# Products of constants ahead of the sorts and the sets on TensorE

## The chip, the cores and the metric

The kernel runs on one core of one Trainium2 chip. The metric is the device time of one execution in microseconds (us). The engines are named as in the profile: PE is TensorE (PEld its weight loads), DVE VectorE, ACT ScalarE, POOL GpSimd, SP SyncE, which issues most DMAs. PE's clock is granted at one of two levels, 2.4 GHz (1.00 in the profile) and 1.2 GHz (0.50).

## The reference

Two transformer layers over x of 8 x 256 x 256. Layer 0 is a cross attention over a context, a self attention and a mixture of eight experts; layer 1 is a cross attention and a second expert layer, which is the part around the change. In it, tokens are taken in groups of 32; in each group each of 128 (expert, set) pairs chooses one token, that token runs through a small two-layer net of the pair, and the results are added back to the tokens:

```python
logits = einsum('bntd,des->bntes', grouped, Wc) + bc
logits = logits + tie
perm = (logits == max(logits, axis=-3, keepdims=True))
permuted = einsum('bntd,bntes->bnesd', grouped, perm)
inner = relu(einsum('bnesd,esdf->bnesf', permuted, W1) + b1)
result_permuted = einsum('bnesf,esdf->bnesd', inner, W2) + b2
result = einsum('bnesd,bntes->bntd', result_permuted, perm)
```

Here n counts the groups (64 in all with the batch), t the 32 tokens of one, e and s the 128 pairs, d the 256 features and f the 32 features of the small net.

## The kernel before

It is one program of five instruction streams, one for each engine, which meet through semaphores. A list of steps, worked out once, gives the order; each engine runs through the list and does its share of each step. So the order on PE is fixed: an instruction that waits holds up all that stand behind it. The rows of x are worked on in blocks of two tiles of 128 rows, eight blocks per attention, numbered 0 to 7, 8 to 15 and 16 to 23 over the three attentions.

The steps around the change, in the order of the program:

- The last attention (blocks 16 to 23) ends, for each block, with p1 (L850, spreads the inverse sums), p2 (`project_out`, L861 in f32 and L863 in bf16), a layernorm on DVE and POOL, ft (`front_turn`, L954, transposes it), fw (`front_choice`, L963, the choice logits), fm (three DVE operations that find the maxima) and fp (`perm_turn`, L971, transposes the choice). ACT copies the results of ft, fw and fp. In the list `last_order` these steps of the last two blocks, 22 and 23, stand between the sorts.
- `sort(b, k)`, gp in the list, b = 0 to 7, k = 0, 1: it gathers the chosen rows of block b by 24 products of 32 rows (L991), in two passes of 12; the second pass waits for the first (`wait_ge("gp", done + 2)`). It writes one of two buffers of PSUM, `PS`, in turn. Two copies (gc, 512 columns each) bring a buffer to G in SBUF; for b below 2 ACT makes both (L1217), else ACT one and DVE the other (L1568). A sort waits until the copies of the sort two before it have freed its buffer.
- `sets_up(b)`, e1, b = 0 to 3: 128 products of 128 rows by 32 columns (L1007) into one of three banks MB. It waits for all copies of the sorts. DVE adds the bias (L1574), ACT applies relu.
- `sets_down(n)`, e2, n = 0 to 7: 64 products of 32 rows (L1029) into four banks, even n into `PS`, odd n into U and MB. DVE (L1584) and ACT (L1229) copy them out; group n waits for the copies of group n - 2, which used its banks.
- Then transposes (L1042) and the products that add the results back (L1053).

The kernel has products of constants elsewhere: `keep_busy`, L1069, a matrix product of two constant tiles into `PS[0]`, behind steps listed by hand, among them eight behind the last `sets_down`. `idb` is the identity in bf16, `lo` a bf16 constant of 128 x 256; both are in SBUF long before the sorts. A `Gate` leaves out a wait that the engine has passed already.

Of the kernel before, what the change touches and what calls it, by code (L numbers as in the profile page):

```python
# [192 lines left out]
def down_on(g, j):  # L193


    return "a" if j == 0 or j == 1 and g in (0, 2, 4) else "b"


def downs(engine, g):

    return sum(down_on(i, j) == engine for i in range(g + 1) for j in range(4))
# [80 lines left out]
def count(what, *key):  # L282
    return NO[what][key]


def copies(engine, b, k):

    return sum(copy_on(*s[1:]) == engine for s in STEPS if s[0] == "gc" and s[1:3] <= (b, k))
# [47 lines left out]
BANKS = Ring(3, bank_users())  # L336
# [97 lines left out]
def build(nc, D, out, stack):  # L434
# [39 lines left out]
    idb = g0.new("idb", [128, 128], BF)  # L474
    vec = g0.new("vec", [128, 160])
    cst = g0.new("cst", [128, 176])
    lo = g0.new("lo", [128, 2, 128], BF)
# [145 lines left out]
    def set_bank(g, j):  # L623

        return ((U, MB[0], MB[1], MB[2])[j][:, :] if g % 2 else PS[j // 2][:, 512 * (j % 2):512 * (j % 2) + 512])
# [23 lines left out]
    def bank(*step):  # L649
        return MB[BANKS.of[step]]  # L650

    def pair(*step):
        return PS[PAIRS.of[step]]
# [70 lines left out]
    def tensor(e):  # L724
        g = Gate(e, sems)
# [240 lines left out]
        def perm_turn(n):  # L966
# [4 lines left out]
                i = e.transpose(b[:, 128 * tt:128 * tt + 128], perm[:, 8 * p + 4 * tt:8 * p + 4 * tt + 4, :], idf[:, :])  # L971
            i.then_inc(sems["pt"], 1)

        def sort(b, k):
            ps, done = pair("gp", b, k), 4 * (count("gp", b, k) - 1)
            g.wait_ge("perm_turned", b + 1)
            g.wait_ge("f_turned", 2 * (b + 1))
            g.wait_ge("fz", b + 1)
            g.wait_ge("fl", b + 1)
            for signal in PAIRS.free["gp", b, k] or ():  # L980
                g.free(signal)

            for pair_of in ((0, 2), (1, 3)):
                if pair_of[0]:
                    g.wait_ge("gp", done + 2)
                for tt in range(2):
                    t = 2 * b + tt
                    for part in range(3):
                        z = z2[:, t, :] if part == 2 else z01[:, t, part, :]
                        for r in pair_of:  # L990
                            i = e.matmul(ps[:, 512 * (r // 2) + 256 * (r % 2) + 128 * tt:][:, 0:128],  # L991
                                         z[32 * r:32 * r + 32, 128 * k:128 * k + 128], pT[32 * r:32 * r + 32, t, :],
                                         start=part == 0, stop=part == 2)
                            if (tt, part) == (1, 2):
                                i.then_inc(sems["gp"], 1)

        def sets_up(b):
            m = bank("e1", b)
            g.wait_ge("d_v1", 16)
            g.wait_ge("sorted_a", copies("a", 7, 1))  # L1000
            g.wait_ge("sorted_b", copies("b", 7, 1))
            g.free(BANKS.free["e1", b])
            for q in range(8):
                for j in range(4):
                    s = 16 * (2 * b + q // 4) + 4 * j + q % 4
                    for k in range(2):
                        i = e.matmul(m[32 * j:32 * j + 32, 64 * q:64 * q + 64], v1[:, k, s, :], G[:, k, s, :],  # L1007
                                     start=k == 0, stop=k == 1)
            i.then_inc(sems["e1"], 1)

        def sets_down(n):
            b, half = GROUPS[n] // 2, GROUPS[n] % 2
            banks = [set_bank(n, j) for j in range(4)]
            g.wait_ge(f"d_v2{(0, 1, 2, 0)[b]}", 32 if b in (0, 3) else 16)
            g.wait_ge("relu", b + 1)
            if n == 0:
                g.wait_ge("sorted_a", copies("a", 7, 1))
                g.wait_ge("sorted_b", copies("b", 7, 1))
            elif n == 1:
                g.wait_ge("up", 4)  # L1020
                g.wait_ge("u_copied", 48)
            else:
                g.wait_ge("down", downs("b", n - 2))
                g.wait_ge("down_a", downs("a", n - 2))

            for q in range(4):
                for k in range(2):
                    for j in range(4):
                        i = e.matmul(banks[j][:, 128 * q + 64 * k:128 * q + 64 * k + 64],  # L1029
                                     v2[32 * j:32 * j + 32, 4 * GROUPS[n] + q, 128 * k:128 * k + 128],  # L1030
                                     Tmp[b][32 * j:32 * j + 32, 4 * half + q, :], start=True, stop=True)
                        if (q, k) == (3, 1):
                            i.then_inc(sems["e2"], 1)
# [911 lines left out]
    with nc.Block() as block:  # L1945
        block.tensor(tensor)
        block.scalar(scalar)
        block.vector(vector)
        block.gpsimd(gpsimd)
        block.sync(sync)  # L1950
# [100 lines left out]
```

## Time and profile before

| | us |
|---|---|
| median of 3 runs | 826.19 |
| the runs | 825.30 to 828.41 |
| the profiled execution | 823.46 |
| its span | 821.5 |

All times below are from the profiled execution, counted from the start of its span. "Busy" counts the time an engine's instructions take; the granted clock is the mean over a stretch; the stage table has the engines in the order PE, PEld, DVE, ACT, POOL. In a timeline, equal instructions in a row are merged: start, time from the first one's start to the last one's end, engine, line, operation, what it writes and reads, shape and count; in brackets the engine's idle time just before and what ended it. "issue" there means that the engine waited for nothing that the profile shows. An f32 product of the program stands as two instructions in the trace. Products overlap, so the time of a merged row holds the last one's own latency.

### The profile page before, as it was taken

Reading aid. Unit: us, or ns where it says so; the run is one execution under the profiler, and the core shown is the slowest. Engines: PE = TensorE matmul, PEld = TensorE weight load, DVE = VectorE, ACT = ScalarE, POOL = GpSimd, SP = SyncE. Lnnn points to the kernel's source line nnn. Section 1 sums busy time; section 2 is a strip of 40 time slices with the busy share of each in tenths; the row PEclk is TensorE's granted clock in tenths of the full one; section 3 lists DMA queues with packets and bytes.
Section 4 is the critical chain, followed back from the end, with each engine's and each line's share of the span. In section 5 each row is a group of like instructions: output and inputs, shape, how many; then the busy total and the mean of one; then the engine's idle time right before and its main releaser. Section 6 shows DMA issues by size and latency. Waiting matters only on the chain.

```text
span 821.5 us, 17575 instructions
## 1 busy us (share of the span) xinstructions
PE 715.4 (87%) x6672; PEld 547.8 (67%) x6672; DVE 469.9 (57%) x1206; ACT 363.3 (44%) x671; POOL 251.6 (31%) x320
## 2 busy tenths in 40 slices
PE   8777988889988999887999999989887887888898
PEld 6544655556666666577988899977655565555775
DVE  4757777777788798571221221224557677746375
ACT  4355656445656655602232322210454546545233
POOL 6722434323443321212120210005433434332140
PEclk9988999999999999999999999999979899977899
DMA  9697666755654584339647476502658363043302
GB/s 192 100 208 133 109 89 93 94 93 94 86 84 78 82 184 148 143 129 325 229 115 244 120 239 192 182 20 69 103 93 121 54 91 54 29 169 162 106 16 90
DMA packets 60534, 101.90 MB, mean 124 GB/s; under 512 B 7278, under 2 KB 50734, under 8 KB 55440
## 3 DMA queue, kind: packets, MB, share of 16 engines
q1 hardware_dynamic: 58020, 95.29, 51.1%
q0 software_dynamic: 1872, 5.11, 3.1%
q8 instruction: 54, 0.88, 0.5%
q10 hardware_dynamic: 560, 0.38, 0.2%
q14 instruction: 28, 0.23, 0.1%
HBM read 55.22 MB, written 7.21 MB: 76 GB/s over the span
## 4 chain that ended last, share of the span: by engine, by line
PE 52%; DVE 18%; ACT 8%; DMA 5%; issue 5%; POOL 5%; another core or an unknown queue 3%; SPq 3%; ACTq 0%; POOLq 0%; DVEq 0%
PE MB L754 8%; PE PS L934 8%; PE U L945 7%; DVE nma L1339 5%; PE MB L861 5%; PE U L837 4%; PE MB L796 3%; PE MB L777 3%; DMA mw<-in_mw 2%; PE PS L819 2%; SPq L1820 2%; PE MB L1042 2%; PE PS L991 2%; DVE nmb L1339 1%
## 5 line engine op out<-in xcount | busy, mean ns | idle before, releaser
L1339 DVE TENSOR_REDUCE nma<-MB 128x2 f32<-128x512 f32 (+1 forms) x192 | 122.2, 671 | 38.5 <-PE MB L796 38.5
L1157 ACT ACTIVATE Pa<-PS 128x1024 f32<-128x1024 f32 (+1 forms) x96 | 97.8, 1025 | 32.9 <-PE PS L819 31.5
L934 PE MATMUL PS<-mzT,mw 128*128 128x128 f32 x736 | 86.3, 276 | 3.9 <-DMA mw<-in_mw 3.9
L945 PE MATMUL U<-mw,mdT 128*128 x368 | 85.3, 386 | 4.6 <-DVE mdT L1531 2.3
L796 PE MATMUL MB<-QKa 99*128 99x120 bf16 (+1 forms) x512 | 70.9, 250 | 19.2 <-DVE nma L1339 4.9
L934 PEld LDWEIGHTS PS<-mzT,mw 128*128 128x128 f32 x736 | 84.1, 192 | 5.0 <-DMA mw<-in_mw 4.9
L1539 DVE TENSOR_TENSOR yt<-U,mb 128x256 f32<-128x256 f32 x23 | 9.8, 424 | 131.7 <-PE U L945 131.7
L945 PEld LDWEIGHTS U<-mw,mdT 128*128 128x128 f32 x368 | 69.4, 194 | 14.3 <-issue 5.6
L796 PEld LDWEIGHTS MB<-QKa 99*128 99x128 bf16 x512 | 37.7, 100 | 50.8 <-DVE nma L1339 13.5
L1632 POOL TENSOR_TENSOR mv<-mv,vec 128x2 f32<-128x2 f32 (+1 forms) x40 | 30.6, 765 | 113.9 <-DVE mv L1296 62.0
L819 PE MATMUL PS<-QKa 101*128 101x256 bf16 (+1 forms) x384 | 58.8, 277 | 2.1 <-DMA QKa<-mTa 2.1
L837 PE MATMUL U<-Pa,Vaa 128*32 128x256 f32 (+1 forms) x768 | 56.9, 399 | 2.0 <-ACT Pa L1157 2.0
L1179 ACT ACTIVATE mzT<-MB,vec 128x128 f32<-128x128 f32 x46 | 18.6, 456 | 88.7 <-PE MB L918 88.7
L1676 POOL DMA_INDIRECT zt<-hb,rows_of x23 | 22.0, 956 | 109.7 <-PE MB L918 97.8
L754 PE MATMUL MB<-zTa,W 128*128 128x256 f32 x192 | 48.3, 396 | 6.6 <-ACT zTa L1095 3.5
L1641 POOL TENSOR_TENSOR rqa<-tqa,spa 128x512 f32<-128x512 f32 (+1 forms) x28 | 32.4, 1158 | 69.0 <-ACT tqa L1136 46.4
L1339 DVE TENSOR_REDUCE nmb<-MB 128x4 f32<-128x480 f32 x64 | 39.8, 645 | 18.0 <-PE MB L796 17.3
L819 PEld LDWEIGHTS PS<-QKa 101*128 101x128 bf16 (+1 forms) x384 | 38.5, 112 | 9.9 <-issue 3.5
L754 PEld LDWEIGHTS MB<-zTa,W 128*128 128x128 f32 x192 | 35.3, 194 | 14.3 <-ACT zTa L1095 4.3
L1648 POOL TENSOR_TENSOR spa<-rqa,spa 128x512 bf16<-128x512 f32 (+1 forms) x28 | 32.6, 1163 | 33.2 <-ACT spa L1144 33.0
L1157 ACT ACTIVATE Pb<-PS 120x1024 f32<-120x1024 f32 x32 | 32.8, 1026 | 14.0 <-PE PS L819 13.8
L1189 ACT ACTIVATE mdT<-PS,vec 128x128 f32<-128x128 f32 x92 | 26.4, 372 | 28.4 <-PE PS L934 28.0
(227 smaller groups left out, 1388.3 us busy)
## 6 DMA issues: line engine op xcount, KB each, us to landing
mw<-in_mw SPq DMA_DIRECT2D x31, 1024.0 KB, 6.5
QKa<-spa SPq DMA_DIRECT2D x144, 128.0 KB, 4.8
Qb<-spb SPq DMA_DIRECT2D x48, 128.0 KB, 4.3
Oa<-Uba SPq DMA_DIRECT2D x16, 256.0 KB, 2.6
v<-in_v SPq DMA_DIRECT2D x1, 4096.0 KB, 13.4
v<-in_v SPq DMA_DIRECT2D x4, 1024.0 KB, 10.6
yb<-yt SPq DMA_DIRECT2D x23, 128.0 KB, 1.7
QKa<-spa SPq DMA_DIRECT2D x24, 120.0 KB, 4.0
```

The source lines that it names most:

```text
L754: i = e.matmul(b[:, 256 * half:256 * half + cols], w[:, k, 128 * half:128 * half + 128], rhs[:, k, :], start=k == 0, stop=k == 1)
L796: i = e.matmul(b[:, keys * j:keys * j + keys], Q[0:99, h0 + j, 128 * qt:128 * qt + 128], K[0:99, h0 + j, 0:keys], start=True, stop=True)
L819: i = e.matmul(ps[0:keys, c:c + 256], K[0:101, h, keys * kt:keys * kt + keys], Q[0:101, h, :], start=True, stop=True)
L837: i = e.matmul(U[32 * j:32 * j + 32, 256 * gg:256 * gg + 256], V[0:keys, kt, 8 * half + 4 * gg + j, :], p[0:keys, c:c + 256], start=kt == ...
L861: e.matmul(b[:, 256 * tt:256 * tt + 256], o[:, half, 128 * tt:128 * tt + 128], W.o[:, half, :], start=half == 0, stop=False)
L934: i = e.matmul(ps[:, 128 * f:128 * f + 128], w[:, k, 128 * f:128 * f + 128], zz[:, k, :], start=k == 0, stop=k == 1)
L945: i = e.matmul(U[:, 0:256], mdT[j % 2][:, f, :], w2[:, bass.ds(expert[j], 1), f, :], start=f == 0, stop=f == 7)
L1157: e.activation(p[0:keys, :], ps[0:keys, :], ACT.Exp, scale=0.25).then_inc(sems["exp"], 1)
L1339: e.tensor_reduce(A.nm[qt][:, h0:h0 + heads], b[:, 0:heads * keys].rearrange("p (h s) -> p h s", h=heads), AX.X, ALU.max, negate=True).the ...
L1632: e.tensor_tensor(rs[r][:, 0:w], ve[r][:, 0:w], mhalf[:, 0:w], ALU.pow).then_inc(sems["rs"], 1)
L1641: e.tensor_tensor(r, f32, hi, ALU.subtract).then_inc(sems["split_r"], 1)
L1648: e.tensor_tensor(low, whole(what, n)[1], mid_, ALU.subtract).then_inc(sems["split_l"], 1)
```

## The change

A new helper, `keep_clock(bank, n)`, puts n products of idb and lo, 256 columns each, into the first half of a bank that is about to be filled. It is called with 3 in each of the four sorts of b = 0 and 1 and with 2 in each of the other twelve, behind the waits that free the buffer; with 8 in the first `sets_up`, ahead of its waits for the sorts' copies; and with 2 in each `sets_down`, behind its waits. The step's own products overwrite what they wrote. In `sets_up` the wait that frees the bank now stands ahead of the other waits. That is 60 products, 36 + 8 + 16, and nothing else is changed; no other engine has a new instruction or a new wait.

```diff
+        def keep_clock(bank, n):
+
+            g.wait_ge("idb", 1)
+            g.wait_ge("d_lo", 16)
+            for _ in range(n):
+                e.matmul(bank[:, 0:256], idb[:, :], lo[:, :, :].rearrange("p a n -> p (a n)"), start=True, stop=True)
+
         def sort(b, k):
...
             for signal in PAIRS.free["gp", b, k] or ():
                 g.free(signal)
+            keep_clock(ps, 3 if b < 2 else 2)
 
             for pair_of in ((0, 2), (1, 3)):
...
         def sets_up(b):
             m = bank("e1", b)
+            g.free(BANKS.free["e1", b])
+            if b == 0:
+                keep_clock(m, 8)
             g.wait_ge("d_v1", 16)
             g.wait_ge("sorted_a", copies("a", 7, 1))
             g.wait_ge("sorted_b", copies("b", 7, 1))
-            g.free(BANKS.free["e1", b])
...
                 g.wait_ge("down_a", downs("a", n - 2))
+            keep_clock(banks[0], 2)
```

## Rows read from the trace of the kernel before

**Rows 1.** Page: busy time of PE and its weight loads; granted clock; queue 8

```profile
PE 715.4 (87%) x6672; PEld 547.8 (67%) x6672; DVE 469.9 (57%) x1206; ACT 363.3 (44%) x671; POOL 251.6 (31%) x320
...
PEclk9988999999999999999999999999979899977899
...
q8 instruction: 54, 0.88, 0.5%
```

**Rows 2.** Stage table: stretch us, busy us (x) per engine, PE clock, DMA share, GB/s

```profile
729.00:732.50 3.50, 2.67 (x80) 2.00 (x80) 3.21 (x10) 2.08 (x4) 0.70 (x1) 1.00 0.73 227
...
732.50:739.00 6.50, 6.41 (x43) 4.55 (x36) 3.27 (x9) 3.34 (x6) 1.15 (x1) 0.50 0.93 403
...
739.00:749.50 10.50, 8.24 (x139) 5.50 (x137) 8.78 (x21) 5.75 (x11) 4.28 (x4) 0.98 0.75 314
...
749.50:761.00 11.50, 10.04 (x170) 7.01 (x170) 5.52 (x8) 5.38 (x8) 0.00 (x0) 0.50 0.01 3
...
774.00:790.50 16.50, 15.67 (x518) 15.02 (x513) 11.95 (x19) 6.28 (x11) 10.30 (x10) 1.00 0.24 84
```

**Rows 3.** PE's timeline, 726 to 740: start us, us, operation, count [idle before]

```profile
726.86 1.13 PE L861 MATMUL MB<-W,Ob 128*128 128x256 f32 x4 [0.28 <-DVE Ob L1378]
...
728.81 0.27 PE L863 MATMUL MB<-W,lo 96*128 96x256 bf16 x1
...
729.01 1.86 PE L991 MATMUL PS<-pT,z 32*128 32x128 bf16 x48
...
735.30 2.07 PE L861 MATMUL MB<-W,Ob 128*128 128x256 f32 x4
...
739.09 0.40 PE L863 MATMUL MB<-W,lo 96*128 96x256 bf16 x1
```

**Rows 4.** Chain of waits, 728 to 762: shares by line

```profile
by line: PE PS L991 47.5%; PE MB L861 13.7%; ACT G L1217 7.2%; issue 5.8%; PE MB L954 4.4%; PE MB L963 3.1%; PE MB L971 2.9%; PE MB L1007 2.5%; DVE Yz L1316 2.2%; POOL mv L1632 2.1%; DVE st L1291 1.9%; PE MB L863 1.9%; PE MB L850 1.6%; DVE 
```

**Rows 5.** PE's timeline, 743 to 751

```profile
743.55 0.66 PE L954 MATMUL MB<-idf,Yz 128*128 128x128 f32 x4 [1.04 <-DVE Yz L1316]
...
744.14 1.10 PE L991 MATMUL PS<-pT,z 32*128 32x128 bf16 x24
...
749.50 1.67 PE L991 MATMUL PS<-pT,z 32*128 32x128 bf16 x24 [0.75 <-ACT G L1217]
```

**Rows 6.** All engines' timeline, 751 to 760: the sorts' copies and one weight load

```profile
751.24 0.73 ACT L1217 ACTIVATE G<-PS 128x512 f32<-128x512 f32 x1 [1.82 <-PE PS L991]
...
753.52 0.73 ACT L1217 ACTIVATE G<-PS 128x512 f32<-128x512 f32 x1 [1.31 <-PE PS L991]
...
754.51 0.58 PEld L991 LDWEIGHTS PS<-pT,z 32*128 32x128 bf16 x12 [0.21 <-issue]
...
756.32 0.73 ACT L1217 ACTIVATE G<-PS 128x512 f32<-128x512 f32 x1 [0.94 <-PE PS L991]
...
759.07 0.73 ACT L1217 ACTIVATE G<-PS 128x512 f32<-128x512 f32 x1 [0.90 <-PE PS L991]
```

**Rows 7.** PE's timeline, 761 to 777: the sets' products and stops

```profile
761.17 7.49 PE L1007 MATMUL MB<-G,v 128*32 128x64 f32 x331 [1.06 <-ACT G L1217]
...
769.37 2.04 PE L1007 MATMUL MB<-G,v 128*32 128x64 f32 x128 [0.71 <-issue]
...
773.10 1.08 PE L1007 MATMUL MB<-G,v 128*32 128x64 f32 x53 [1.69 <-issue]
...
776.92 0.33 PE L1029 MATMUL MB<-etmp,v 32*128 32x64 f32 x3 [0.37 <-issue]
```

**Rows 8.** PE's timeline, 790: products of constants already there

```profile
790.57 1.05 PE L1069 MATMUL PS<-lo,idb 128*128 128x256 bf16 x8
```

**Rows 9.** Timelines of PE and DVE in sets_down

```profile
782.40 2.04 PE L1029 MATMUL PS<-etmp,v 32*128 32x64 f32 x64
...
786.45 1.97 PE L1029 MATMUL PS<-etmp,v 32*128 32x64 f32 x64
...
782.67 1.89 DVE L1584 TENSOR_TENSOR R<-MB,c 128x512 f32<-128x512 f32 x3 [0.86 <-PE MB L1029]
```

## The prediction

> **What bounds the kernel now.** I read the page first, then the table of stages, then the engines' timelines with the chain of waits beside them. On the page the reader is to see that PE has work in 87% of the span, and that the line of granted clock dips only in places, one of them near the end [rows 1]. The table of stages puts numbers on that dip. From 729.0 to 732.5 us the clock was 1.00, and PE ran almost nothing but line 991, the sorts' products of 32 rows. Then it was 0.50 (1.2 GHz) up to 739, 0.98 behind the full-size products of line 861, and 0.50 again from 749.5 to 761, where line 991 ran alone once more. The engine was no less occupied there than elsewhere (10.04 us of 11.5). From 774 to 790.5, with the sets' small products, it stayed at 1.00 [rows 2]. So it is the sorts that go to half rate, and these two stretches alone are 18 us at it. The chain of waits between 728 and 762 lies on line 991 for 47.5% and on line 861 for 13.7% [rows 4]. This is the stretch in which a faster TensorE is worth something. Ahead of 729 nothing is changed, and behind 790.5 nothing either.
>
> **What a product of constants costs.** Eight of the same kind, line 1069, take 1.05 us, of which the last one's own 0.27 is drain, so 0.78 / 7 = 0.11 us each [rows 8]. At half rate I take twice that. They use all 128 rows of the array, and the sorts 32. From line 863 to the first sort PE needs 0.20 us instead of 0.11, so changing over costs 0.09 [rows 3]. The way back has no clean row. Its bounds are nothing (the next weights are loaded beside the running product) and 0.16 (all of the 0.27 that is not spacing); I take 0.09, the nearest row. Two products between two sorts then cost 0.22 + 0.18 = 0.40, three 0.51; where the engine waits for a buffer, or already runs 128 rows, one change less.
> By the Trainium skill, page TensorEngine Tiling (Array Packing), section Key Properties, changing the tiling mode drains TensorE. That speaks against this change, and the trace agrees that there is a price. At a full drain of 0.16 instead of 0.09, some 28 changes on the path would make the sum 2 us worse, about 827.7.
>
> **Stage A, 729 to 749.5.** Sixteen sorts, (b, k) with b = 0 to 7. At full rate one takes 1.10 us with its drain, two in a row 1.86 [rows 3, 5]: the second hides 0.34 beside the first, which a group of products between them forbids. Issue alone is 1.10 - 0.22 = 0.88. Sort (0,0) starts 0.33 late, and so do ACT's copies of it. Sort (1,0) waits for these, then issues its own three products and a change (0.42). Followed through (1,1), PE reaches p1 of row 23 some 0.7 late though at full rate. p1 and ft at full rate give 0.2 back, so p2 starts 0.5 late, at 735.8. p2 itself took 2.22 at full rate for row 22 (726.86 to 729.08) and 4.19 at half rate for row 23 (735.30 to 739.49) [rows 3], so 1.97 is saved, and p2 ends 1.45 early. Of this, 0.3 is lost to ACT, whose later copies hold up the transposed rows that DVE's next cast waits for. So the statistics of row 23, its normalization and ft come 1.15 early. The products of (2,0) and (2,1) lie in PE's idle 1.04 ahead of ft [rows 5]. Those of (3,0) stand ahead of fw of row 23: +0.22. Those of (3,1) and (4,0) fit into the 0.75 that PE idles ahead of (4,1) [rows 5]; without that cover they would cost 0.5. Sum of A: **-0.95**.
>
> **Stage B, 749.5 to 761.17.** Before, 4.02 us from (4,1) to the copies of (5,0), then 2.80 and 2.75 per pair of sorts, then 2.10 to the first product of the sets [rows 5, 6, 7]. After, at full rate: 0.31 for two products and a change, 0.88, 0.31 for the transpose of row 23, 0.31, 1.10, 0.07 to the copies (751.17 to 751.24): 2.98, so -1.04. A pair takes PE 2 x (0.88 + 0.40) = 2.56; the other loop, one buffer's products, sort, copy (0.73) and release (0.26, 754.25 to 754.51), takes 0.31 + 1.10 + 0.07 + 0.73 + 0.26 = 2.47 and is just covered. So PE bounds the pair, and only 0.24 and 0.19 are won. The last sort ends 0.17 later behind the one before it. Sum of B: **-1.3**. The eight products ahead of the sets (0.88 and a change) lie beside the last copies, for PE idles 1.06 there [rows 7]; at half rate they would stand out by 0.7. The free of their bank, now taken earlier, is long given.
>
> **Stage C, the sets' first products.** Here the faster clock should win little. PE stops twice for nothing that the trace names, 128 products apart and at full rate: it resumes at 769.37 and at 773.10, 3.73 us apart, though 128 products take 2.04 with their drain [rows 7]. 128 products with their weight loads are 256 instructions. The page has 2 x 6672 of them on PE, and a queue for instructions with 54 packets of 16 KB, some 247 instructions each [rows 1]. So I read the stops as PE's program arriving in pieces, none sooner than about 3.75 us after the one before. The 44 added products (36 and 8) move the borders of the pieces 44 products ahead. Counted from the first set product, borders that lay at 8.2, 11.9 and 15.75 us come at about 7.0, 10.75 and 14.5, but 44 products earlier in the program, which then take 1.3 more, and two more groups (0.4). Sum of C: **+0.45**, from -0.5 to +1.2.
>
> **Stage D, sets_down.** The clock is 1.00 already [rows 2], so its products buy nothing. A group of 64 takes 2.04 with its drain of 0.27, so about 1.8 of issue, and two 3.65. A pair takes 4.05 (782.40 to 786.45), because the odd group waits for DVE's three copies of 1.89 [rows 9]. With its products a group takes 0.40 more, a pair 4.45 on PE, while DVE's loop grows by 0.31 only, to 4.36. So PE bounds, at +0.40 for each of three pairs and 0.1 for the first: **+1.3**, from 0.7 (no change of mode) up to 1.9.
>
> **Sum.** -0.95 - 1.3 + 0.45 + 1.3 = -0.5 us on the profiled execution's 823.46 (span 821.5 and 2.0 around it). The median of the runs shown is 826.19, 2.7 above it, and the runs lie 3.1 apart; I put the same difference on it: **825.7 us**. The profiled execution fell to half rate early in A. One that doesn't fall there has nothing to win in A, and pays about 0.9 there: +1.35 in all, 827.5. That lies in the range.
>
> **The rivals.** *The clock falls all the same.* Then all prices double: a sort in B takes 0.18 + 0.44 + 0.18 and its own 1.45 (1.67 less a drain) [rows 5], a pair 4.5 instead of 2.78. B gets 5.5 longer, A 2.7, the eight products 0.7, D 1.3: 836.4. It decides as soon as B alone stays at 1.2 GHz: then 832.7. For it: PE was not idle when the clock fell, so being busy isn't enough. Against it: rows of 128 x 128 products (line 861) brought it back, and the small products of stage D kept it.
> The Trainium skill, page TensorE: Matmul & The Clock Gate, in the table Why this matters for your kernels, asks for no long idle gaps between bursts of products. By that alone the clock should not have fallen from 749.5 on, where PE was busy for 10.04 us of 11.5; the trace disagrees.
> *Changing modes is free where products queue up* (loads beside running products): some 14 groups on the path lose 0.18 each, -2.5: 823.2. For it, the 0.09 may be the wait of the sort's first load. *The stops in C go away*, because they came from the transfer of weights beside them and not from PE's program: 512 products at full rate are 7.3 us (by 1.83 for 128) instead of the 12.1 of my sum, and a stop of 1.3 in the first group of sets goes with them: 825.7 - 6.1 = 819.6. Against it: the stops come a fixed number of products apart.
>
> **How the numbers follow.** Forecast, with the clock held and its gain spent on the products, 0.62; not falling in A before, 0.10; free changes 0.14; no stops 0.06; clock lost 0.08. The range leaves out the last two: 822.8 to 828.5, free changes at its low end, full drains and a kind start of A at its high end. Half a per cent, 4.1 us, is about what a measurement of this kernel can tell: faster needs the stops gone, or free changes with luck (0.09), slower needs the clock lost (0.08).
>
> **What would show it.** The stage table after should have 1.00 from 729 to the last set, p2 of row 23 at about 2.2 us, pairs of sorts 2.5 to 2.6 us apart, the stops of 3.7 us period still among the first sets' products, but 44 products earlier, and pairs of sets_down 4.4 to 4.6 apart. Half rate anywhere from 729 to 761 makes it wrong upwards; sets_up in under 9 us, downwards.

## The result, and the profile after

The changed kernel is slower: 847.45 us (median; 837.3 to 855.5) beside 825.75 for the kernel before, a ratio of 1.0156 with a 95% interval of 1.0097 to 1.0215. Ratios leave out the executions that lie over 1.5% above the fastest of the same kernel, while the medians given here are over all of them. The forecast was 825.7.

The page of the changed kernel's profiled execution (837.3 us, span 835.3), to be read beside [rows 1]: PE's busy time has grown by 14.8 us for 60 more products, and the dip of the clock has moved to the end.

```profile
PE 730.2 (87%) x6732; PEld 557.3 (67%) x6732; DVE 470.2 (56%) x1206; ACT 363.3 (43%) x671; POOL 251.8 (30%) x320
...
PEclk9988999999999999999999999999989999998569
```

The stage table of after, cut where the clock changes (columns as in [rows 2]; the granted clock is the third from the right):

```profile
722.50:753.40 30.90, 28.51 (x451) 18.86 (x450) 20.24 (x45) 15.86 (x28) 7.01 (x7) 1.00 0.55 219
753.40:760.20 6.80, 6.71 (x142) 5.03 (x144) 1.44 (x2) 1.45 (x2) 0.00 (x0) 0.50 0.01 2
760.20:773.90 13.70, 9.19 (x484) 8.37 (x476) 2.78 (x5) 2.63 (x5) 0.00 (x0) 1.00 0.46 157
773.90:808.00 34.10, 33.91 (x485) 29.38 (x485) 13.98 (x22) 6.85 (x13) 11.32 (x11) 0.50 0.01 2
```

The sorts now run at full rate up to 753.4: the first part did its work. But from 773.9 to 808.0 the clock is 0.50, through nearly all of sets_down, which in the kernel before ran at 1.00 [rows 2]. PE was busy for 33.91 of those 34.10 us: once at half rate, being busy did not bring it back.

PE's timeline of after, answering to [rows 3, 5, 7, 9] (L979 the new products, L999 the sorts, L1017 sets_up, L1040 sets_down):

```profile
732.68 1.13 PE L861 MATMUL MB<-W,Ob 128*128 128x256 f32 x4 [0.41 <-DVE Ob L1389]
...
734.63 0.27 PE L863 MATMUL MB<-W,lo 96*128 96x256 bf16 x1
...
746.58 0.38 PE L979 MATMUL PS<-lo,idb 128*128 128x256 bf16 x2
746.89 1.11 PE L999 MATMUL PS<-pT,z 32*128 32x128 bf16 x24
747.93 0.39 PE L979 MATMUL PS<-lo,idb 128*128 128x256 bf16 x2
...
749.29 0.39 PE L979 MATMUL PS<-lo,idb 128*128 128x256 bf16 x2
...
755.59 1.89 PE L979 MATMUL MB<-lo,idb 128*128 128x256 bf16 x8
757.40 5.62 PE L1017 MATMUL MB<-G,v 128*32 128x64 f32 x288
764.20 2.07 PE L1017 MATMUL MB<-G,v 128*32 128x64 f32 x128 [1.18 <-issue]
767.65 1.62 PE L1017 MATMUL MB<-G,v 128*32 128x64 f32 x96 [1.39 <-issue]
...
769.53 1.11 PE L1040 MATMUL PS<-etmp,v 32*128 32x64 f32 x29
...
772.57 1.33 PE L1040 MATMUL PS<-etmp,v 32*128 32x64 f32 x35 [1.94 <-issue]
...
778.53 3.69 PE L1040 MATMUL PS<-etmp,v 32*128 32x64 f32 x64
...
786.85 3.69 PE L1040 MATMUL PS<-etmp,v 32*128 32x64 f32 x64
```

The reader is to see a third stop, 1.94 us long, 29 products into sets_down, where the kernel before had one of 0.37 [rows 7]; behind it a group of 64 takes 3.69 instead of 2.04, and a pair of groups 8.32 (778.53 to 786.85) instead of 4.05 [rows 9].

The 13.7 us between the two spans, by stage: ahead of the sorts -3.45 (725.56 instead of 729.01; nothing is changed there); to sort (4,1) -1.09 (19.40 instead of 20.49); on to the first set product +0.77 (12.44 instead of 11.67); sets_up -1.13 (11.81 instead of 12.94); sets_down with its products +17.28 (769.21 to 802.95, 33.74 instead of 16.46); behind it +1.35. The whole loss is sets_down. The -3.45 is no gain of the change: the same program, profiled once more (e12), came to its sorts at 734.90 instead of 725.56, and took 109.8 us from there to the end of its span, beside 109.7 here and 92.5 before.

### The profile page after: what moved, and what is told of

Its sections match the earlier page's. It is cut to its first block, busy times and chain, and to the rows that moved or that the text cites. A ratio compares the mean times of both kernels' runs of the same rounds, so it can differ in the third digit from the quotient of the medians.

```text
span 835.3 us, 17694 instructions
## 1 busy us (share of the span) xinstructions
PE 730.2 (87%) x6732; PEld 557.3 (67%) x6732; DVE 470.2 (56%) x1206; ACT 363.3 (43%) x671; POOL 251.8 (30%) x320
## 4 chain that ended last, share of the span: by engine, by line
PE 59%; DVE 17%; ACT 8%; issue 5%; POOL 4%; DMA 4%; SPq 2%; ACTq 0%; DVEq 0%; POOLq 0%
PE U L945 9%; PE PS L934 9%; PE MB L754 8%; DVE nma L1350 5%; PE MB L861 4%; PE U L837 4%; PE MB L796 3%; PE MB L777 3%; PE PS L819 2%; PE PS L1080 2%; PE MB L1053 2%; PE PS L999 2%; PE PS L1040 2%; PE U L1040 2%; DVE nmb L1350 1%
## 5 line engine op out<-in xcount | busy, mean ns | idle before, releaser
L1080 PE MATMUL PS<-lo,idb 128*128 128x256 bf16 x318 | 39.5, 276 | 0.9 <-issue 0.8
L1168 ACT ACTIVATE Pb<-PS 120x1024 f32<-120x1024 f32 x32 | 32.9, 1027 | 12.4 <-PE PS L819 12.2
```

Of the source, the lines that this page charges most:

```text
L1080: e.matmul(PS[0][:, 0:256], a, b, start=True, stop=True)
L1168: e.activation(p[0:keys, :], ps[0:keys, :], ACT.Exp, scale=0.25).then_inc(sems["exp"], 1)
```

## Experiments

A border is the place where one piece of PE's program ends; a stop is the time for which PE stands idle there with no releaser in the profile. The theory after the result: the added products move the borders, a stop comes to lie in sets_down, the clock falls behind it and does not return there. The rivals: the added products themselves cost the time; the clock would have fallen in sets_down anyway. Each comparison is with runs of the kernel before on the same chip; its medians there were 829.86 (the first four experiments), 826.92, 829.58 (four each), 829.92 and 831.56 (three each). The kernel before itself spread from 818.5 to 841.8 us on these chips, with a mean granted clock of 0.964 and 0.933 at the two ends. Only one of its executions has a profile, so where the longer ones lost their clock, in sets_down or elsewhere, is not shown.

Four edits recur. A: n of the 106 products of constants at 556 us are cut into halves, 2 n more PE instructions for the same columns. B: two products between a sort's two passes. C: fillers in sets_up. D: the last transfers of weights later.

Edit A is not free, though the expectations below take it as free. The halves use up PE's pieces sooner, PE stops there too, and in all its profiles but e6's the clock falls there. PE's timelines of before and of e1 (n = 44), from the first of these products to the next step (L734):

```profile
556.83 11.74 PE L1069 MATMUL PS<-lo,idb 128*128 128x256 bf16 x106
569.24 0.66 PE L734 MATMUL MB<-idf,zb 128*128 128x128 f32 x4 [0.68 <-issue]
```
```profile
559.11 9.44 PE L1071 MATMUL PS<-lo,idb 128*128 128x128 bf16 x128
...
575.71 1.06 PE L734 MATMUL MB<-idf,zb 128*128 128x128 f32 x4
```

This stretch takes 12.2 to 12.4 us in every profile without A, 15.3 to 17.1 with n = 44, 17.7 to 18.0 with n = 48 and 17.6 to 21.3 with n = 80 to 96. How much of that reaches the end can't be told exactly, for the sorts begin at 725.6 to 734.9 without A and at 725.9 to 745.0 with it (medians 728.9 and 732.6). The medians and ratios of runs with A contain it. So profiles are also compared from the first instruction of the sorts' step to the end of the span, which leaves it out: 92.5 us before, 109.7 after.

**The border alone, and the border put back.** e1_shift_only is the kernel before with edit A, n = 44, and no product ahead of anything:

```diff
-            for _ in range(IDLE[step]):
-                e.matmul(PS[0][:, 0:256], a, b, start=True, stop=True)
+            for k in range(IDLE[step]):
+                halves = ((0, 128), (128, 256)) if step == ("se", NTILE - 1) and k < 44 else ((0, 256),)
+                for c, d in halves:
+                    e.matmul(PS[0][:, c:d], a, b[:, c:d], start=True, stop=True)
```

> The kernel before, with no product ahead of sorts or sets. Only 44 of the 106 products of constants that already fill a wait at about 556 us are each split into two halves of 128 columns: the same columns, but 88 more PE instructions, as many as stand ahead of the sets in the changed kernel. Theory S (the loss comes from where the pieces of PE's program end): borders move by 44 products, a stop falls some 31 products into the first group of sets_down, the clock falls there and stays at 0.50 to the end of sets_down; 836 to 841 us. Rival P (the added products and their changes of mode cost the time): nothing changes, 826 us, stops at the places of before.

Measured: 841.04, ratio 1.0154 [1.0092, 1.0215]. PE's timeline (sets_up L1007, sets_down L1029), then its stage table from the fall on:

```profile
777.56 1.62 PE L1007 MATMUL MB<-G,v 128*32 128x64 f32 x97 [1.42 <-issue]
779.11 1.11 PE L1029 MATMUL PS<-etmp,v 32*128 32x64 f32 x31
782.21 1.65 PE L1029 MATMUL PS<-etmp,v 32*128 32x64 f32 x33 [1.98 <-issue]
```
```profile
782.80:813.50 30.70, 30.70 (x497) 29.27 (x497) 14.21 (x23) 7.44 (x13) 11.33 (x11) 0.50 0.03 9
```

88 instructions some 220 us earlier, and nothing in the sorts or the sets, bring the stop and the fall. From the sorts on e1 takes 105.2 us: 12.7 more than before, of the 17.2 that after takes more. Another 4.2 us of e1 are A's own, ahead of the sorts. e2_after_unshifted is the changed kernel with n = 84 (168 instructions), which brings the borders back to where the kernel before has them:

```diff
+                halves = ((0, 128), (128, 256)) if step == ("se", NTILE - 1) and k < 84 else ((0, 256),)
```

> The changed kernel with all its products; 84 of the 106 products at about 556 us are split into halves, 168 more instructions, so that with the 88 added ones the borders of the pieces of PE's program lie where they lay before (256 instructions are one piece). S: stops at set products 331 and 459 as before, clock 1.00 in sets_down, 826 to 829 us (its 16 products cost about 1.3 to 2 there). P: no better than the changed kernel, 837 to 840 us.

Measured: 832.96, ratio 1.0032 [0.9963, 1.0100]; one of the four executions took 859.72. That is 4 us above what was expected, and A's stretch took 18.4 us here, 6.0 more than before. PE's timeline has all its stops in sets_up, and sets_down at full rate:

```profile
780.72 1.08 PE L1017 MATMUL MB<-G,v 128*32 128x64 f32 x52 [1.66 <-issue]
...
782.05 2.01 PE L1040 MATMUL PS<-etmp,v 32*128 32x64 f32 x64
...
786.70 1.57 PE L1040 MATMUL PS<-etmp,v 32*128 32x64 f32 x48
```

From the sorts on e2 takes 94.3 us. So the place of the border makes 15.4 of the 17.2 us by which after is longer there (12.7 by e1, which has no products), and the 60 products 1.7, as long as the clock holds in sets_down. In sets_down alone they cost 1.8 (781.73 to 799.98, 18.25 instead of 16.46).

**Parts of the change.** e3_no_down is the changed kernel without its products in sets_down:

```diff
-            keep_clock(banks[0], 2)
```

> The changed kernel without the 16 products in sets_down; those of the sorts and the 8 ahead of the first set stay, so the borders ahead of sets_down are the changed kernel's. S: the stop still falls in the first group of sets_down, the clock still falls and stays at 0.50, only the products' own 0.5 us each group are saved: 832 to 836 us. P: the products in sets_down were the cause, clock 1.00 there, 825 to 827 us.

Measured: 839.59, ratio 1.0127 [1.0058, 1.0196], where 832 to 836 was expected. The stop of 2.26 us in sets_down and the fall (at 786.5, for 27.3 us) are there without them. And the clock also fell among the sorts, with their products in place (stage table):

```profile
742.00:772.00 30.00, 29.11 (x376) 18.89 (x377) 10.47 (x18) 10.12 (x17) 2.31 (x2) 0.50 0.17 71
```

A pair of sorts then took 4.40, and sorts to sets 40.5 us. Up to there it is the changed kernel's program, which held the clock to 753.4 in its own profile: products ahead of the sorts don't secure it.

e4_sorts_unshifted has the products of the sorts and the eight ahead of the sets alone, with the borders put back (the edit of e3 and edit A, n = 84).

> Products ahead of the sorts and the first set only, none in sets_down, and 84 of the products at about 556 us split, so that the borders lie where they lay before. S and P both: clock 1.00 in sets_down. What it tells apart is the worth of the sorts' products alone: 824 to 825.5 us if stages A and B are won as predicted (-2.2, with +0.5 given back at the first sets), 826 to 827 us if the clock still falls among the last sorts.

Measured: 827.29, 831.59, 852.66 and 853.37, median 842.12, ratio 1.0013 [0.9932, 1.0093], where 824 to 827 was expected. In the profile of the first the clock held until 760.3, and sorts to sets took 31.4 us, counted from the first sort, instead of 32.16. From the sorts on it takes 92.6 us, as before: ahead of the sorts, the products cost what the clock gives.

Executions of 851.8 to 859.7 us, like the two here, came in after (2 of 4), e2 (1 of 4) and e11 (2 of 7), which all have products ahead of the sorts, and in e9 (1 of 12), which has none; e3 and e12 have such products and had none of these. The place of the border doesn't explain them, for e2 and e4 have it back. The only one with a profile, e11's, was at half rate from 744.8, among the sorts, to 775.5, and again in sets_down.

**Between the passes.** e5_between_passes (B, and A with n = 96, so that the borders are those of before):

```diff
                 if pair_of[0]:
+                    keep_clock(ps[:, 256:512], 2)
                     g.wait_ge("gp", done + 2)
```

> The kernel before with products of constants in the sorts alone, and not ahead of them: two stand between a sort's two passes, written to the half of the bank that the second pass is about to fill. 96 products of constants at 556 us are cut into halves, so that the borders of PE's pieces lie where the kernel before has them, and sets_up and sets_down are as before. Theory 'hidden in the wait': the second pass waits for the first to drain anyway (1.10 us for a sort at full rate, of which 0.88 is issue), so most of the products' 0.4 lies in that wait; the clock is at 1.00 from the sorts' start to the last sort, pairs of sorts are 2.2 to 2.4 us apart instead of 2.78, sorts to sets take 29 to 30 us instead of 32.2, and the time is 1.5 to 3 us under before (822 to 825 where before is 825.75). Theory 'the products cost what the clock gives wherever they stand': pairs 2.6 to 2.75 apart and the time within 1 us of before, as in the run with the sorts' products ahead of the sorts and the borders unshifted. If the clock falls among the sorts all the same, a pair is about 4.4 apart and the time 834 or more.

Measured: 836.01, ratio 1.011 [1.003, 1.019]: the sorts beat the expectation, and the time missed it. PE's timeline of two sorts (L999) of one pair and the start of the next, then the stage table of the sorts and of the fall:

```profile
750.04 0.51 PE L999 MATMUL PS<-pT,z 32*128 32x128 bf16 x12
750.48 0.39 PE L979 MATMUL PS<-lo,idb 128*128 128x256 bf16 x2
750.81 0.64 PE L999 MATMUL PS<-pT,z 32*128 32x128 bf16 x24
...
752.36 0.51 PE L999 MATMUL PS<-pT,z 32*128 32x128 bf16 x12
```
```profile
727.10:757.90 30.80, 27.59 (x473) 17.79 (x471) 21.56 (x47) 17.15 (x30) 6.96 (x7) 1.00 0.55 220
...
771.50:802.20 30.70, 30.54 (x522) 29.57 (x515) 13.70 (x23) 7.47 (x13) 11.33 (x11) 0.50 0.12 38
```

A pair takes 2.32 (750.04 to 752.36), sorts to sets 27.6 us instead of 32.2. The gain of 4.6 us was then lost in sets_down, which took 10.6 more, behind a stop of 1.97 us that ended 1.0 us ahead of it (769.95); A's stretch took another 8.0 more than before.

**What lets the clock fall.** e6_kick is e1 with 16 products of 128 rows ahead of the second group of sets_down:

```diff
+            if n == 1:
+                keep_clock(banks[0], 16)
```

> The kernel before with the 88 more PE instructions at 556 us that put the third stop into sets_down (alone: 841.04), and one thing more: 16 products of constants of 128 rows ahead of the second group of sets_down, behind the stop. Theory 'half rate there keeps itself up': the clock falls at the stop; the group's 64 products of 32 rows at half rate do not bring it back, but rows of products of 128 by 128 do, as line 861 did in the sorts. Then the half rate ends within some 7 us instead of 30.7, groups behind are 2.0 us apart again instead of 3.4 to 4.2, and the time is 829 to 834. Rival 'sets_down cannot hold the clock behind a stop': it comes back for a moment or not at all and falls again, sets_down takes 28 us or more, and the time is 841 or more.

Measured: 832.15 over ten executions, ratio 1.0064 [1.0014, 1.0114], less than that of e1. But the profiled one (837.63) fell at 773.7, at the end of the stop, and stayed at half rate for 34.1 us, the 16 products included. PE's timeline:

```profile
773.50 2.06 PE L1038 MATMUL PS<-etmp,v 32*128 32x64 f32 x33 [1.44 <-issue]
775.49 3.59 PE L979 MATMUL U<-lo,idb 128*128 128x256 bf16 x16
```

So 3.59 us of them don't always bring it back. Whether they do in the faster executions, no profile shows; this stays open.

e7_late_transfer is e1 with edit D:

```diff
             for b in (1, 2):
-                g.wait_ge("e1", b + 2)
+                g.wait_ge("e2", 4 * b)
                 e.dma_start(v2[:, 8 * b:8 * b + 8, :], D["v2"][:, 8 * b:8 * b + 8, :]).then_inc(sems[f"d_v2{b}"], 16)
```

> The kernel before with the same 88 more PE instructions at 556 us (alone: 841.04), and the last two transfers of the weights of sets_down (1 MB each) each begun four groups of sets_down later, not while sets_up runs out. Theory 'the transfers lengthen the third stop': without them the pieces of PE's program come 3.75 us apart instead of 4.9, the third stop in sets_down is about 1 us instead of 1.9 to 2.3; if the length of the stop is what lets the clock fall, sets_down then stays at 1.00 and the time is 827 to 831, provided that the later weights come in time. Rival 'any stop there lets the clock fall': the third stop is shorter, the clock falls behind it all the same, and the time is 838 to 841. Rival 'the period is its own': the third piece comes 4.9 us after the second with no transfer beside it, and all stays as at 841.

Measured: 838.67, ratio 1.0106 [1.0034, 1.0177]. PE's timeline, and the stage table up to the fall (DMA share and GB/s are its last columns):

```profile
776.32 1.62 PE L1007 MATMUL MB<-G,v 128*32 128x64 f32 x97 [1.42 <-issue]
...
779.87 1.37 PE L1029 MATMUL PS<-etmp,v 32*128 32x64 f32 x33 [0.89 <-issue]
```
```profile
770.00:780.80 10.80, 7.62 (x406) 7.12 (x402) 2.08 (x3) 2.19 (x4) 0.00 (x0) 0.97 0.02 5
```

With the DMA engines idle the third piece came 3.55 us after the second instead of 4.65 in e1, and the stop was 0.89 instead of 1.98. The clock fell all the same (780.8, for 27.3 us). The transfers lengthen the stop; the shorter one does the same harm.

e8_shift_96 is the kernel before with edit A, n = 96:

```diff
+                halves = ((0, 128), (128, 256)) if step == ("se", NTILE - 1) and k < 96 else ((0, 256),)
```

> The kernel before with 96 instead of 44 products of constants at 556 us cut into halves: 192 more PE instructions instead of 88, the same columns. Theory 'where the border lies': with 192 the borders of PE's pieces lie at products 107, 235, 363 and 491 of sets_up, and the next one deep in sets_down, by when it has been delivered; so three or four stops in sets_up, none early in sets_down, sets_down at 1.00 in 16 to 18 us, and the time is 826 to 831. Rival 'more instructions cost': 192 are worse than 88, so 841 or more. Rival 'halves lower the clock at 556 us': a time above 830 with the loss at 556 us and none in sets_down.

Measured: ten executions, three from 825.1 to 828.4 and seven from 834.5 to 843.9, median 836.35, ratio 1.0023 [0.9967, 1.0079], where 826 to 831 was expected. The rival "halves lower the clock at 556 us" is true beside the theory: A's stretch took 20.7 us instead of 12.4, with the clock at 0.67 from 565 to 575 us. There is no stop in sets_down, but one of 1.69 us that ended 0.57 us ahead of it (781.11; sets_down from 781.68), and in the profiled execution (841.14) the clock fell at 783.5 for 27.3 us. A stop just ahead is enough, in some executions.

**Filling the stops.** e9_fill_only is the kernel before with edit C, twelve products of 512 columns into a buffer that sets_down fills later:

```diff
                         i = e.matmul(m[32 * j:32 * j + 32, 64 * q:64 * q + 64], v1[:, k, s, :], G[:, k, s, :],
                                      start=k == 0, stop=k == 1)
+                if b and q % 2:
+                    e.matmul(PS[0][:, 0:512], idb[:, :], z01[:, 0, :, :].rearrange("p a n -> p (a n)"), start=True, stop=True)
```

> The kernel before with one product of 128 by 128 by 512 columns behind every 16 program products of sets_up, from its second block on: twelve in all, written to a buffer that sets_down fills later. They take the place of the stops: 128 trace products at full rate take 1.83 us, four fillers some 1.2 to 1.6 with the changes of mode, which comes near the 3.45 to 3.75 us in which a piece of PE's program arrives. Theory 'the stops at the end of sets_up let the clock fall in sets_down': idle gaps of PE there fall from 0.7 to 2.2 us to under 0.7, sets_up is as long as before within 1 us (12.0 to 13.8), the clock is 1.00 through sets_down (16.3 us), and every run is near the best ones of before, so 1 to 4 us under its median. Rival 'small products alone let it fall': the clock falls in sets_down in some runs as in the kernel before, time at or up to 2 us over before. Rival 'the fillers just cost': sets_up 14.5 us or longer.

Measured: 837.51, ratio 1.0115 [1.007, 1.016]. The stops in sets_up are gone, but sets_up took 15.6 us instead of 12.9, and the 24 instructions moved a border to the end of the first group of sets_down (L1031):

```profile
776.50 2.01 PE L1031 MATMUL PS<-etmp,v 32*128 32x64 f32 x63
779.30 0.32 PE L1031 MATMUL PS<-etmp,v 32*128 32x64 f32 x1 [0.79 <-issue]
```
```profile
780.00:802.50 22.50, 22.50 (x433) 22.50 (x432) 10.47 (x17) 4.56 (x8) 9.63 (x10) 0.50 0.03 10
```

A stop of 0.79 us, and half rate behind it. e10_between_fill (A with n = 96, B and C) has the same border, 0.33 us long, and held:

> The products between the two passes of each sort (sorts to sets 27.6 us instead of 32.2 in the earlier run) together with the twelve fillers in sets_up. Theory 'stops': without them the clock holds in sets_down, which takes 16.3 to 17 us instead of 26.7, and the gain of the sorts is kept: 3 to 5 us under before, ratio 0.994 to 0.996. Rival: the clock falls in sets_down all the same, and the time is 831 to 836 as without the fillers.

```profile
772.71 0.32 PE L1039 MATMUL PS<-etmp,v 32*128 32x64 f32 x1 [0.33 <-issue]
```
```profile
759.10:817.00 57.90, 52.04 (x1175) 39.57 (x1171) 32.29 (x57) 18.32 (x31) 11.34 (x11) 1.00 0.22 75
```

Measured: 827.21, ratio 0.9988 [0.9947, 1.0029], where 0.994 to 0.996 was expected; two of twelve executions at 839. e11_after_fill (the changed kernel and C) and e12_after_again (the changed kernel itself) stand together:

> The changed kernel with the twelve fillers in sets_up. Theory 'stops': the third stop, 29 products into sets_down, shrinks from 1.94 us to under 0.7, the clock stays at 1.00, sets_down takes 17.5 us (pairs 4.5) instead of 33.1, and the time is 825 to 829, some 10 us or more under the changed kernel in this batch. Rival 'its own products and small rows lose the clock anyway': 836 or more. In between (830 to 835): the fall is only less frequent.

> The changed kernel itself, beside the one with fillers and on the same chip. From its first result: 1.010 to 1.022 times before, half rate from a stop in sets_down on for about 30 us. If the fall were a matter of that first execution alone, most runs would lie at the time of before.

Measured: 842.63, ratio 1.0178 [1.0111, 1.0245], and 843.86, ratio 1.0197 [1.0132, 1.0262]. The fillers did not help: in e11 (the profiled execution took 855.84) the third stop is still 1.54 us, 17 products into sets_down. Both fell behind their stops, for 37.5 and 34.1 us; the changed kernel's loss is no matter of one execution.

**Other ways to a short stop.** e13_fill_late has A (n = 96), B, C and D; e15_before_late has D alone.

> Products between the passes of the sorts, the twelve fillers in sets_up, and the last two transfers of weights begun one and two groups into sets_down. Without the late transfers the stop that is left, 47 products into sets_down, took 0.60 us and the clock held in the profiled run; 2 of 12 executions were near 839. Theory 'a long stop in sets_down lets the clock fall, and transfers beside it make it longer': the stop is gone or under 0.4 us, the clock holds in nearly every execution, the time is 818 to 826 with none at 835 or more, ratio 0.990 to 0.996. Rival 'the fall is a chance of its own': some executions near 839 as before, median 825 to 828.

> The kernel before with only the last two transfers of weights begun one and two groups into sets_down. Theory 'the kernel before loses the clock in sets_down in some of its executions, and the transfers beside the pieces of its program are why': the stops in sets_up are shorter (1.69 us becomes about 1.2), fewer executions at 833 or more, median 2 to 5 us under before. Rival 'they play no part before': the same spread and the same median within 1 us. If the weights come late, sets_down stands still ahead of its fifth group, and the time is over that of before.

Measured: 832.63, ratio 1.0035 [0.999, 1.0081], and 835.13, ratio 1.0065 [1.002, 1.0111]. Both expectations failed: in the profiled executions the later transfers only harm another place. (That of e13 is its longest, 843.79, and its sorts begin at 745.0, 16.0 us later than before; from there on it takes 96.6 us.) PE's timeline of e13 (L1039), where now PE itself waits for the weights, and of e15 (L1029), where the border in the fourth group has them beside it:

```profile
796.38 3.69 PE L1039 MATMUL PS<-etmp,v 32*128 32x64 f32 x64 [1.42 <-DMA v<-in_v]
```
```profile
782.09 0.21 PE L1029 MATMUL U<-etmp,v 32*128 32x64 f32 x1 [1.95 <-issue]
```

The clock fell at these two places (796.1 and 782.5) and nowhere earlier in sets_down. e13 also shows that the stop need not come from the program's pieces.

e14_fill_shift has A with n = 48, B and C; e16_fill_shift_again is the same kernel once more:

> Products between the passes and the twelve fillers, with 48 instead of 96 products of constants at 556 us cut into halves: 96 PE instructions less ahead of sets_down, so the border that lay 47 products into sets_down lies 95 products in, in its second group. Theory 'place of the border': there PE has run behind the fillers and 1.5 groups of sets_down, which take about as long as a piece, so the stop is under 0.6 us, the clock holds, and the time is 820 to 827. Rival: the stop is longer there (0.8 us or more), the clock falls in most executions, and the time is 833 or more.

> The version with the products between the passes of the sorts, twelve fillers in sets_up and 48 products at 556 us cut into halves, once more: first it was 825.01, ratio 0.9969 [0.9931, 1.0006]. If the sorts' gain of some 4.5 us less 1.3 for the fillers is real, the ratio is 0.994 to 0.998 again and about one execution in ten loses the clock in sets_down; if it was luck, 1.000 or more.

Measured: 825.01, ratio 0.9969 [0.9931, 1.0006], and 824.59, ratio 0.9877 [0.979, 0.9963]; the medians are 4.9 and 7.0 us under those of before, though e14's interval takes in 1. One of e14's twelve executions took 836.09, and three of e16's six 829.0 to 834.9, where one in ten was expected to lose the clock; none of these has a profile. The two profiles have no stop in sets_down above 0.22. e18_fill_shift_no_sorts (C, and A with n = 80) has the same borders, and nothing in the sorts:

> The twelve fillers in sets_up and 80 halved products at 556 us, with nothing in the sorts: the borders of the pieces are those of the version with the products between the passes, and the sorts are those of the kernel before, at half rate. Theory 'the sorts' gain is real once the clock holds in sets_down': this one is 2 to 5 us slower than its sister with the products between the passes, 827 to 831; the stop in sets_down is under 0.7 us and the clock holds in most executions. Rival 'all that sister's gain comes from the clock in sets_down': the two are equal within 1 us.

Measured: 833.22, ratio 1.0103 [1.0065, 1.0141]. The stage tables of e16 and e18, sorts, sets_up and sets_down:

```profile
728.70:756.20 27.50, 24.62 (x453) 16.02 (x452) 20.91 (x46) 16.56 (x29) 6.13 (x6) 0.99 0.61 245
756.20:771.40 15.20, 13.61 (x522) 11.18 (x528) 2.27 (x4) 1.89 (x3) 0.00 (x0) 0.90 0.21 70
771.40:787.50 16.10, 15.64 (x516) 15.14 (x516) 11.82 (x20) 6.44 (x12) 10.26 (x10) 1.00 0.22 72
```
```profile
732.20:763.90 31.70, 27.07 (x421) 18.89 (x420) 20.81 (x46) 16.61 (x29) 6.13 (x6) 0.72 0.53 213
763.90:779.30 15.40, 13.38 (x522) 10.96 (x528) 2.27 (x4) 1.89 (x3) 0.00 (x0) 0.91 0.21 69
779.30:795.50 16.20, 15.57 (x517) 15.05 (x517) 12.02 (x20) 6.64 (x12) 10.26 (x10) 1.00 0.22 72
```

The sorts' gain is real: 4.2 us between the two spans lie there, sets_up and sets_down are equal within 0.3. Another 3.5 lie ahead of the sorts (start at 728.66 and 732.15), where the two differ by 32 halved products: A's stretch takes 17.8 us in e16 and 21.3 in e18. So the products between the passes give some 4 us (89.6 and 93.9 from the sorts on), and not the 8.6 between the two medians.

e17_shift_no_fill is e16 without the fillers (A with n = 48, and B):

> The same without the twelve fillers. The borders of PE's pieces then lie at about products 380 and 508 of the 512 of sets_up, the second with a stop of some 2 us right ahead of sets_down. Theory 'a long stop in or shortly ahead of sets_down lets the clock fall': half rate from there on for 27 us or more in most executions, 831 to 837. Rival 'only the place of the border in sets_down matters': it holds, and the time is 819 to 825, for the fillers' 1.3 us are saved.

Measured: 826.94, ratio 0.9932 [0.9886, 0.9978]; seven of twelve executions from 820.0 to 828.4, five from 834.7 to 845.1, so neither the theory nor the rival holds for all. In the profiled one (span 826.4) the stops lie in sets_up, the last 0.34 us ahead of sets_down, and the clock held:

```profile
772.20 2.04 PE L1015 MATMUL MB<-G,v 128*32 128x64 f32 x128 [1.42 <-issue]
775.65 2.04 PE L1015 MATMUL MB<-G,v 128*32 128x64 f32 x128 [1.42 <-issue]
779.11 0.41 PE L1015 MATMUL MB<-G,v 128*32 128x64 f32 x5 [1.42 <-issue]
779.45 2.01 PE L1037 MATMUL PS<-etmp,v 32*128 32x64 f32 x64
```

The profiled executions side by side (longest stop in sets_down; the time of sets_down from its first product to the first transpose; the time from the sorts' step to the end of the span):

| kernel | stop in sets_down, us | half rate in sets_down | sets_down, us | from the sorts on, us |
|---|---|---|---|---|
| before, e10, e14, e16, e18 | 0.37 or less | no | 17.8 to 18.5 | 89.6 to 93.9 |
| e2, e4, e17 | none; 1.42 to 1.94 in sets_up | no | 18.1 to 20.0 | 88.7 to 94.3 |
| e5, e8 | none; 1.97 and 1.69 just ahead | yes | 29.1, 28.0 | 99.6, 103.3 |
| e9, e7 | 0.79, 0.89 | yes | 28.4, 29.1 | 106.1, 103.3 |
| after, e1, e3, e6, e11, e12 | 1.39 to 2.26 | yes | 30.2 to 36.3 | 105.2 to 122.6 |
| e13, e15 | 1.42, 1.95, in a later group | yes, from there on | 25.2, 27.5 | 96.6, 102.6 |

## Why the prediction was wrong

**The price of the products was right, that of a pair too low.** Two products and a change of mode took 0.31 (746.58 to 746.89), as priced. The sort behind them took 1.04 up to the next products, not 0.97, so pairs are 2.72 instead of 2.56 apart.

**Stage A was right:** p2 of row 23 took 2.2 us (732.68 to 734.90), and the stage gave -1.09 where -0.95 was forecast. That the sum came so close is in part luck: p2 began 0.83 late instead of 0.5 and ended 1.14 early instead of 1.45, and the steps behind it lost less than was forecast.

**Stage B was wrong in sign,** +0.77 for -1.3: about 0.5 from the pairs, and the rest from half rate at 753.4, which doubled the last sort and the eight products. The rival "the clock falls all the same" was not empty: e3, e11 and, at the very end of the sorts, after, e2, e4 and e12 show it; its price of 4.5 for a pair fits e3's 4.40. Its chance of 0.08 was too low. e4 and e5 show what the sum could not: the place of the products, ahead of the sort or in its own wait, is worth 3.8 us (31.4 and 27.6 from sorts to sets).

**Stage C read the cause rightly.** The borders came 6.80, 10.25 and 15.17 us after the first set product (forecast 7.0, 10.75, 14.5), 44 products earlier, and the first two of them cost 2.57 us together, 2.40 before. The third was 4.92 us behind the second, not 3.75: 1 MB transfers ran beside it, and e7 shows that they account for about 1.1 of it.

**Stage D is the step that failed:** "The clock is 1.00 already, so its products buy nothing", and with it the +1.3. C moved a stop of 1.94 us into sets_down, and D took the clock there as given. I priced a stop by its length alone; it costs the rate of all small products behind it, +17.3 instead of +1.3. e1 shows that the moved border alone lets the clock fall, e2 that the fall is undone with it. The price of D's products was right for the clock that it assumed: in e2, at 1.00, they cost 1.8 (forecast 0.7 to 1.9), and the first pair of groups took 4.65 (782.05 to 786.70; forecast 4.45). The list of what would show the forecast wrong had half rate from 729 to 761, and not behind it.

The prediction held the Trainium skill's advice against idle gaps (TensorE: Matmul & The Clock Gate, table Why this matters for your kernels) to be contradicted by the sorts. For after that stands: its clock fell at 753.4, and PE's longest pause in the nine us ahead was 0.14. Of the kernel before I misread it. The 10.04 of 11.5 us are what PE was busy behind its fall; just ahead, PE had stood idle for 0.75 us up to 749.50 [rows 5]. In sets_down the trace goes further than the advice, which speaks of gaps longer than any stop here: the clock fell behind 0.79 us. I set the rule aside for the whole kernel on the evidence of one stage.

**The range** took a difference of 4 us as measurable. With twelve executions it is (intervals of 0.4 to 0.5% to either side), with four it is not (0.6 to 0.8%). Both its ends held the clock in sets_down at 1.00.

## What to carry to other kernels

Instructions that are added to a dense stretch of small products move every later border at which the program itself arrives; look where the stops will lie, and what clock the work behind them needs, before pricing their length. Products that only keep the clock up belong into a wait that the engine has anyway (between two passes of one step), not ahead of the step. The version that follows from both, with products between the passes, fillers in sets_up and the border moved out of the first group of sets_down, measured 825.01 and 824.59 beside 829.92 and 831.56 of the kernel before. It moves the border by edit A with n = 48, whose stretch takes some 5 us more than in the kernel before; a cheaper way to move it was not tried. An edit that is meant to move something and change nothing else has to be timed where it stands, too.

## What the runs showed of the hardware

- PE's stops follow the count of instructions, not the work: borders moved by the number of instructions added far ahead (e1: 88 for 44 products). Where short instructions used a piece up, the next came 3.45 us later with the DMA engines idle (share 0.02: e17, 772.20 to 775.65), 3.46 with a share of 0.58 (e17, to 779.11), and 4.65 and 4.92 beside 1 MB transfers with shares of 0.92 and 0.90 (e1, after).
- Full rate in sets_down is kept by the same products that do not restore it: 64 products at 2.04 us a group kept it in the kernel before, and at half rate PE busy for 33.91 of 34.10 us did not bring it back in after. It came back only past the end of sets_down (808.0; first transpose at 805.03), in e1 too (813.5; 809.56). The products of sets_up, which use 128 rows, did bring it back in every profile without fillers: in after at 760.2, with sets_up from 757.40, and in the kernel before at 766.5, so that its half rate reached past 761 into the sets.
- Behind a stop in sets_down of 0.79 us or more every profiled execution fell; with 0.38 or less none did (before 0.37, e10 0.33, e15 0.38 ahead of its longer one). With stops only ahead of sets_down, some executions fell and some did not (e5 and e8 against e2, e4 and e17): e4 held behind a stop of 1.94 us that ended 1.0 us ahead of sets_down, e5 fell behind one of 1.97 that ended as far ahead. What decides between them is open.
